# A message-passing layer on one core: the one-hots compare with a row of numbers in PSUM, and the places are counted in one bank

## The chip, the core and the metric

The kernel runs on one core of a Trainium2 chip. The metric is the time of one execution on the device, in microseconds. A core has TensorE (PE in the profile; PEld is its weight load), VectorE (DVE), ScalarE (ACT), GpSimd (POOL) and SyncE (SP), which run side by side and wait for each other through semaphores, and DMA queues that move data between HBM and SBUF. TensorE writes to PSUM, a small memory of eight banks of 512 float32 numbers in each of 128 partitions. VectorE and ScalarE read it; in this kernel GpSimd and the DMA queues work on SBUF and HBM alone.

## What is computed

The inputs are 12,500 nodes with 128 features and 400,000 edges, sorted by destination, each with 20 attributes and a weight. Here `src` is `idx_i`, by which the sums are taken, and `dst` is `idx_j`, whose row is fetched.

```
h   = relu(layernorm(x)) @ W_in2f.T
Wij = smu(edge_attr_20 @ W_f1.T + b_f1) @ W_f2.T + b_f2      # per edge, 128 wide
Wij = Wij * edge_weight[:, None]
msg = h[dst] * Wij
agg = segment_sum(msg, src, 12500)
out = x + smu(agg @ W_o1.T + b_o1) @ W_o2.T + b_o2
```

`smu(x)` is a smooth activation made of `x` and `x * erf(...)`; the kernel builds it from one Gelu and one multiply-add.

## The kernel before

The edges are padded to 784 **units** of 512 edges (4 tiles of 128). 112 units make a **round**, and there are 7 rounds. A node is in one of 112 **buckets** by its row number modulo 112. For each unit, messages are computed and scattered to HBM, sorted by bucket (`sorted_rows`); for each round and bucket, 640 sorted rows are loaded again one round later and summed by node on TensorE with a second one-hot (a **segment**; 784 of them, `SEG_LAG` = 120 units behind). A prologue makes `h`, a last part makes the output from `agg`.

What happens to a unit n, with the names of the profile:

- TensorE makes `p_z` (line 926), ScalarE its Gelu (583), VectorE `act` (762).
- VectorE makes `pick` (766), the one-hot with which TensorE fetches `h[dst]` from a window (`p_h`, 944); ScalarE weighs it into `hg` (594).
- VectorE makes `onehot` (`bucket_of`, 771): 4 tiles of 112 columns, the row of numbers 0 to 111 (`iota_bf`, bf16, SBUF) compared with each edge's bucket (`node_l`, SBUF). TensorE multiplies it with triangular matrices (`rank` and `counted`, 950 and 967), which adds to a running count in the bank `p_pos` where the next free place of each bucket stands. VectorE picks each edge's place out of it (`places`, 785) and adds a correction (`row_numbers`, 793, writes `row_idx`).
- TensorE makes `p_w` (931, 933), VectorE multiplies it with `hg` into `msg` (779).
- GpSimd issues four indirect DMAs (`scatter`, 491), one for each tile, that write `msg` to the rows `row_idx`. `msg` and `row_idx` have four slots (`RING`), so `row_idx` of unit n waits until the scatters of unit n-4 have landed.

For a segment, VectorE makes `seg_hot` (`bucket_hot`, 804): 5 times 112 columns, the same numbers as float32 (`iota`, SBUF) compared with the node number in the loaded rows (`seg`, SBUF). TensorE sums (976), VectorE adds to `agg` (815, in the first round 813).

The order on each engine is written out by hand in a function `step`, run for every unit; `beats` unrolls the first 12 units of each round and loops over the rest. On VectorE a step is `act`, `pick`, `onehot` of unit n; then of unit n-1 `places`, `seg_hot` of a segment, `row_idx`, `agg`, `msg` of unit n-1. Counts of odd and even rounds stand in two banks, `p_pos0` and `p_pos1`. When a round opens, TensorE finishes the old round's count in the old bank and seeds the new one (`rank` with `opens`, 957 to 963); VectorE reads the old bank's totals (`totals`, 796 to 799) once in each round, at the end of the third step.

The eight banks of PSUM are `p_z`, two of `p_w`, `p_h`, two of `p_pos`, two of `p_seg`. The two banks of `p_pos` are used again by the last layer (1030 to 1039, read at 880).

Of the kernel before, what the change touches and what calls it, by code (L numbers as in the profile page):

```python
# [64 lines left out]
def build(nc, n_nodes, n_edges, F, R, t):  # L65
# [27 lines left out]
    with ctx:  # L93
# [3 lines left out]
        def ps(name, shape, dt=F32):  # L97
            return ctx.enter_context(nc.psum_tensor(name, shape, dt))
# [79 lines left out]
        p_z = ps("p_z", [LANES, BANK])  # L178
        p_w = [ps(f"p_w{v}", [LANES, TILES_U, F]) for v in range(2)]
        p_h = ps("p_h", [LANES, TILES_U, F])  # L180
        p_pos = [ps(f"p_pos{v}", [LANES, BANK]) for v in range(2)]
        p_seg = [ps(f"p_seg{v}", [LANES, BANK]) for v in range(2)]

        s_x = sem("s_x")
# [5 lines left out]
        s_pool = sem("s_pool")  # L190
        s_pool2 = sem("s_pool2")
        s_seeds = sem("s_seeds")
        s_u16 = sem("s_u16")
        s_zeros = sem("s_zeros")
        s_zrow = sem("s_zrow")
# [451 lines left out]
        def _(dve):  # L647
# [76 lines left out]
            dve.tensor_scalar(w_o2[:, :], w_o2[:, :], SMU_W, None, ALU.mult).then_inc(s_scaled, 1)  # L724

            dve.wait_ge(s_pool, 5)
            dve.tensor_copy(seeds[0:1, :, :], iota_bf[0:1, :].unsqueeze(1).to_broadcast([1, BUFS, BUCKETS])).then_inc(s_seeds, 1)
            dve.wait_ge(s_win_ld, 32)
            link(dve.tensor_scalar(seed_row[:, :, :], seed_row[:, :, :], float(CAP), (CAP + FILLED) / 2, ALU.mult, ALU.add))
# [25 lines left out]

            loop(dve, phase_a, n_groups, 5)
            dve.wait_ge(s_win_row, 1)

            def smu(n, v):
                wait_for(dve, s_gelu, n, 1, 1)  # L760
# [7 lines left out]

            def bucket_of(n, slot):
                wait_for(dve, s_rank, n, 1, 2 - RING)  # L770
                dve.tensor_tensor(onehot[:, slot, :, :], iota_bf[:, :].unsqueeze(1).to_broadcast([LANES, TILES_U, BUCKETS]),  # L771
                                  node_l[:, bass.ds(n.value(TILES_U), TILES_U)].unsqueeze(2).to_broadcast([LANES, TILES_U, BUCKETS]),
                                  ALU.is_equal).then_inc(s_hot, 1)

# [6 lines left out]
            def places(n, v, slot, rnd):  # L781
                wait_for(dve, s_rank, n, 1, 1)
                wait_for(dve, s_idx, n, 1, -1)
                for k in range(TILES_U):
                    last = dve.tensor_tensor_reduce(out=product[:, k, :], in0=onehot[:, slot, k, :], in1=p_pos[rnd % 2][:, 0:BUCKETS],  # L785
                                                    scale=1.0, scalar=0.0, op0=ALU.mult, op1=ALU.add,
                                                    accum_out=place[:, v, k:k + 1])
                last.then_inc(s_place, 1)
# [6 lines left out]

            def totals(rnd):
                dve.wait_ge(s_total, rnd + 1)
                dve.tensor_tensor(counts[:, rnd, :], p_pos[rnd % 2][0:1, 0:BUCKETS], seed_row[:, rnd % BUFS, :], ALU.subtract
                                  ).then_inc(s_count, 1)

            def bucket_hot(m, v, slot, rnd, ld):
                wait_for(dve, s_segld[slot], ld, 16, 16)
                wait_for(dve, s_seg, m, 1, -1)
                dve.scalar_tensor_tensor(seg_hot[:, v, :, :], seg[:, slot, :, F:F + 1].to_broadcast([LANES, CAP_T, NODE_P]),  # L804
                                         -float(LANES * (rnd + 1)),
                                         iota[:, :].unsqueeze(1).to_broadcast([LANES, CAP_T, NODE_P]), ALU.add, ALU.is_equal
                                         ).then_inc(s_seghot, 1)

            def gather_sum(m, v, rnd, bucket):
# [7 lines left out]
            def step(st):  # L817
                if st.has() and st.v() == 0:
                    wait_for(dve, s_ends[st.q()], st.pair().over(2), 16, 16)
                if st.has():  # L820
                    smu(st.at(), st.v())
                    pick_target(st.at(), st.pair(), st.q(), st.v())
                    bucket_of(st.at(), st.ring())
                if st.has(1):
                    places(st.at(1), st.v(1), st.ring(1), st.rnd_of(1))
                if st.has_seg():
                    bucket_hot(st.seg_at(), st.v(), st.c % SEGS, st.seg_rnd(), st.seg_at().over(SEGS))
                if st.has(1):
                    row_numbers(st.at(1), st.v(1), st.ring(1))
                if st.has_seg(2):  # L830
                    gather_sum(st.seg_at(2), st.v(2), st.seg_rnd(2), st.bucket(2))
                if st.has(1):
                    message(st.at(1), st.v(1), st.ring(1))
                if st.i is None and st.c == 2 and st.rnd >= 1 and st.rnd <= rounds:
                    totals(st.rnd - 1)

            beats(dve, step, 2)

# [38 lines left out]
            def output(g, b, deep):  # L877
                wait_for(dve, s_om, g, 1, 1)
                wait_for(dve, s_xl[deep], g.over(DEEP), 48, 48)
                dve.tensor_tensor(x_out[:, deep, :, :], p_pos[b][0:NODE_P, :].rearrange("p (k n) -> p k n", k=NODE_G),  # L880
                                  x_out[:, deep, :, :], ALU.add).then_inc(s_of, 1)

            for c in range(n_groups + 1):
# [6 lines left out]
        def _(pe):  # L890
# [56 lines left out]

            def counted(slot, rnd):
                for k in range(TILES_U):
                    last = pe.matmul(p_pos[rnd % 2][:, 0:BUCKETS], not_before[:, :], onehot[:, slot, k, :], start=False, stop=False,  # L950
                                     skip_group_check=True)
                return last

            def rank(n, slot, rnd, opens):
                wait_for(pe, s_hot, n, 1, 1)
                wait_for(pe, s_place, n)
                if opens:
                    if rnd > 0:
                        counted((slot - 1) % RING, rnd - 1).then_inc(s_total, 1)
                    if rnd > 1:  # L960
                        pe.wait_ge(s_count, rnd - 1)
                    pe.matmul(p_pos[rnd % 2][:, 0:BUCKETS], step_rows[:, :], seeds[:, rnd % BUFS, :], start=True, stop=False,
                              skip_group_check=True)
                else:
                    counted((slot - 1) % RING, rnd)
                for k in range(TILES_U):
                    last = pe.matmul(p_pos[rnd % 2][:, 0:BUCKETS], before[:, :], onehot[:, slot, k, :], start=False, stop=False,
                                     skip_group_check=True)
                last.then_inc(s_rank, 1)

# [59 lines left out]
            def last_layer(g, b):  # L1030
                wait_for(pe, s_os, g, 1, 1)
                wait_for(pe, s_of, g, 1, -1)
                pe.matmul(p_pos[b][0:NODE_P, :], ones_bf[:, 0:NODE_P],
                          bias_rows[:, B_O2, :, :].rearrange("p k f -> p (k f)"), start=True, stop=False)
                for k in range(NODE_G):
                    last = pe.matmul(p_pos[b][0:NODE_P, k * F:(k + 1) * F],  # L1036
                                     hid[:, b, k * NODE_P:(k + 1) * NODE_P], w_o2[:, :],
                                     start=False, stop=(k == NODE_G - 1))
                last.then_inc(s_om, 1)
# [54 lines left out]
```

## Time and profile before

| | us |
|---|---|
| median of 3 runs | 4690.14 |
| lowest and highest | 4686.88 and 4690.92 |
| profiled execution | 4673.0 |
| its span, first to last instruction | 4671.3 |

The profile is of the one profiled execution, which was 17.1 us faster than the median. It has three stretches: the prologue to 343 us, where GpSimd's first scatter starts; the 784 units, until GpSimd's last scatter ends at 4421 us; and the rest, in which the last round's segments are loaded and summed and the output is made.

### The profile page before, as it was taken

How to read it: one execution, taken by the hardware profiler on the slowest of the kernel's cores; microseconds unless marked ns; L12 is line 12 of the kernel's file. 1: busy time of each engine (PE TensorE's matmuls, PEld its weight loads, DVE VectorE, ACT ScalarE, POOL GpSimd, SP SyncE). 2: the span in 40 equal slices, each digit the busy share in tenths (PEclk: the TensorE clock that was granted, in tenths of full speed). 3: DMA queues.
4: the chain of work that ended last, by engine and by line, in shares of the span. 5: the costliest groups of instructions: out<-in, count | busy, mean ns of one | idle time of the engine just before them, and what ended most of it. 6: DMA issues, size and time to landing. Idle time of an engine off the chain costs nothing.

```text
span 4671.3 us, 120335 instructions
## 1 busy us (share of the span) xinstructions
PE 3674.7 (79%) x32823; PEld 2929.2 (63%) x32823; DVE 3210.1 (69%) x12188; ACT 1518.5 (33%) x4903; POOL 3132.1 (67%) x3158
## 2 busy tenths in 40 slices
PE   0417777788888888888888888888888888888788
PEld 0305555566666666666666666666666666666676
DVE  6406556577777777777777777777777777777665
ACT  0603333333333333333333333333333333333201
POOL 0007777777777777777777777777777777777600
PEclk9759999999999999999999999999999999999999
DMA  8684333355555555555555555555555555555476
GB/s 191 180 189 126 94 96 94 104 156 157 156 155 158 158 159 155 158 158 158 156 155 158 157 155 157 154 155 157 159 156 156 154 158 157 158 156 154 149 216 187
DMA packets 373005, 720.26 MB, mean 154 GB/s; under 512 B 82062, under 2 KB 132900, under 8 KB 372346
## 3 DMA queue, kind: packets, MB, share of 16 engines
q1 hardware_dynamic: 246476, 456.19, 36.2%
q0 software_dynamic: 100352, 207.33, 12.7%
q10 hardware_dynamic: 26082, 55.61, 5.0%
q8 instruction: 44, 0.72, 0.1%
q14 instruction: 51, 0.42, 0.0%
HBM read 450.43 MB, written 268.35 MB: 154 GB/s over the span
## 4 chain that ended last, share of the span: by engine, by line
POOL 33%; DMA 24%; issue 22%; DVE 10%; ACTq 5%; PE 3%; ACT 1%; DVEq 1%; POOLq 1%; SPq 0%
POOL sorted_rows L491 33%; DMA sorted_rows<-msg,row_idx 21%; DVE msg L779 4%; ACTq L536 4%; DMA seg<-sorted_rows 2%; PE p_seg L976 1%; DVE product L785 1%; DMA x_all<-in_x 1%; DVE row_idx L793 1%; DVE onehot L771 1%; DVE agg L815 1%; DVE act L762 1%; POOLq L489 1%; DVE pick L766 1%; PE p_pos L1036 0%
## 5 line engine op out<-in xcount | busy, mean ns | idle before, releaser
L491 POOL DMA_INDIRECT sorted_rows<-msg,row_idx x3136 | 3121.9, 996 | 1249.3 <-issue 1142.3
L976 PE MATMUL p_seg<-seg_hot,seg 128*128 128x112 f32 x7840 | 1031.6, 280 | 323.6 <-DVE agg L815 273.1
L976 PEld LDWEIGHTS p_seg<-seg_hot,seg 128*128 128x128 f32 x7840 | 940.0, 192 | 395.9 <-issue 215.7
L926 PE MATMUL p_z<-attr,w_f 128*128 128x512 f32 x1568 | 862.9, 633 | 262.0 <-DVE act L762 232.7
L587 ACT ACTIVATE msg<-node_p 128x4 f32 (+1 forms) x784 | 163.8, 209 | 2492.9 <-DMA sorted_rows<-msg,row_idx 2492.8
L594 ACT ACTIVATE hg<-p_h,weight 128x128 f32<-128x128 f32 x3136 | 893.1, 373 | 86.5 <-PE p_h L944 58.4
L793 DVE TENSOR_TENSOR row_idx<-place,earlier 128x4 int32<-128x4 f32 x784 | 129.0, 165 | 1108.7 <-DMA sorted_rows<-msg,row_idx 1103.0
L933 PEld LDWEIGHTS p_w<-w_f,act 128*128 128x128 f32 x6272 | 826.9, 192 | 20.7
L933 PE MATMUL p_w<-w_f,act 128*128 128x128 f32 x6272 | 828.5, 275 | 0.0
L950 PEld LDWEIGHTS p_pos<-onehot,not_before 128*128 128x128 bf16 x3136 | 191.7, 98 | 849.1 <-DVE onehot L771 529.4
L944 PE MATMUL p_h<-win,pick 128*128 128x128 bf16 x9408 | 669.6, 222 | 4.1 <-DMA win<-h 4.1
L785 DVE CUSTOM_DVE_ANT_0 product<-onehot,p_pos 128x112 bf16<-128x112 bf16 x3136 | 657.4, 265 | 0.0
L762 DVE SCALAR_TENSOR_TENSOR act<-p_z,gelu 128x512 f32<-128x512 f32 x784 | 535.7, 683 | 160.4 <-ACT gelu L583 149.1
L804 DVE SCALAR_TENSOR_TENSOR seg_hot<-seg,iota 128x560 f32<-128x560 f32 x784 | 578.5, 738 | 84.7 <-DMA seg<-sorted_rows 72.8
L944 PEld LDWEIGHTS p_h<-win,pick 128*128 128x128 bf16 x9408 | 569.5, 100 | 4.5 <-DMA win<-h 4.5
L779 DVE TENSOR_TENSOR msg<-p_w,hg 128x512 f32<-128x512 f32 x784 | 536.5, 684 | 1.4 <-PE p_w L933 1.4
L950 PE MATMUL p_pos<-onehot,not_before 128*128 128x112 bf16 x3136 | 289.3, 216 | 251.0 <-DVE place L785 247.4
L583 ACT ACTIVATE gelu<-p_z 128x512 f32<-128x512 f32 x784 | 467.3, 596 | 59.0 <-issue 41.2
L771 DVE TENSOR_TENSOR onehot<-iota_bf,node_l 128x448 bf16<-128x448 bf16 x784 | 483.9, 617 | 0.0
L926 PEld LDWEIGHTS p_z<-attr,w_f 128*128 128x128 f32 x1568 | 238.8, 192 | 290.8 <-DVE act L762 254.9
L931 PE MATMUL p_w<-bias_rows,ones_bf 128*128 128x512 bf16 x784 | 299.3, 382 | 0.0
L766 DVE TENSOR_SCALAR pick<-ends,win_row 128x512 bf16<-128x512 uint16 x784 | 293.3, 374 | 0.0
(92 smaller groups left out, 1555.1 us busy)
## 6 DMA issues: line engine op xcount, KB each, us to landing
seg<-sorted_rows SPq DMA_DIRECT2D x784, 322.5 KB
ends<-ends SPq DMA_DIRECT2D x392, 256.0 KB
sorted_rows<-msg,row_idx POOLq DMA_INDIRECT x3136
sorted_rows<-zero_rows ACTq DMA_DIRECT2D x12, 3612.0 KB
win<-h SPq DMA_DIRECT2D x392, 96.0 KB
attr<-in_attrT SPq DMA_DIRECT2D x392, 80.0 KB
h<-h_parts SPq DMA_DIRECT2D x28, 336.0 KB, 2.7
x_all<-in_x SPq DMA_DIRECT2D x1, 5376.0 KB
```

The lines of the kernel that those rows point to most:

```text
L491: pool.indirect_dma_start(out=sorted_rows[:, :], out_offset=bass.IndirectOffsetOnAxis(ap=row_idx[:, slot, k:k + 1], axis=0), in_=msg[:, sl ...
L594: last = act.activation(hg[:, v, k, :], p_h[:, k, :], ACT.Copy, scale=weight[:, bass.ds(n.value(TILES_U, k), 1)])
L762: dve.scalar_tensor_tensor(act1[:, v, :], p_z[:, :], SMU_L, gelu[:, v, :], ALU.mult, ALU.add).then_inc(s_smu, 1)
L771: dve.tensor_tensor(onehot[:, slot, :, :], iota_bf[:, :].unsqueeze(1).to_broadcast([LANES, TILES_U, BUCKETS]), node_l[:, bass.ds(n.value(T ...
L779: dve.tensor_tensor(msg[:, slot, :, 0:F], p_w[v][:, :, :], hg[:, v, :, :], ALU.mult).then_inc(s_msg, 1)
L785: last = dve.tensor_tensor_reduce(out=product[:, k, :], in0=onehot[:, slot, k, :], in1=p_pos[rnd % 2][:, 0:BUCKETS], scale=1.0, scalar=0.0 ...
L804: dve.scalar_tensor_tensor(seg_hot[:, v, :, :], seg[:, slot, :, F:F + 1].to_broadcast([LANES, CAP_T, NODE_P]), -float(LANES * (rnd + 1)), ...
L926: pe.matmul(p_z[:, :], w_f1[:, :], attr[:, q, v * UNIT:(v + 1) * UNIT], start=True, stop=True).then_inc(s_z, 1)
L933: last = pe.matmul(p_w[v][:, k, :], act1[:, v, k * LANES:(k + 1) * LANES], w_f2[:, :], start=False, stop=(k == TILES_U - 1))
L944: last = pe.matmul(p_h[:, k, :], pick[:, v, k * LANES:(k + 1) * LANES], win[:, q, part * F:(part + 1) * F], start=(part == 0), stop=(part ...
L950: last = pe.matmul(p_pos[rnd % 2][:, 0:BUCKETS], not_before[:, :], onehot[:, slot, k, :], start=False, stop=False, skip_group_check=True)
L976: last = pe.matmul(p_seg[v][:, 0:NODE_P], seg[:, slot, k, 0:F], seg_hot[:, v, k, :], start=(k == 0), stop=(k == CAP_T - 1))
```

## The change

The two banks of `p_pos` become one bank `p_pos` and one bank `p_iota`. VectorE copies `iota` (float32) into `p_iota` once, in the prologue. `bucket_of` and `bucket_hot` read their row of numbers from `p_iota`, float32 in both; before, `bucket_of` read bf16. Their other operand stays where it was, as do their outputs.

With one bank for the count, TensorE may seed a new round only after VectorE has read the old totals: it waits for `s_count` at every opening of a round but the first, where before it waited for the totals of two rounds ago. VectorE takes the totals one step earlier, between `onehot` and `places` of that step. The last layer alternates between `p_z` and `p_pos`.

```diff
-        p_pos = [ps(f"p_pos{v}", [LANES, BANK]) for v in range(2)]
+        p_pos = ps("p_pos", [LANES, BANK])
+        p_iota = ps("p_iota", [LANES, BANK])
+        p_out = [p_z, p_pos]
...
             dve.wait_ge(s_pool, 5)
+            dve.tensor_copy(p_iota[:, 0:NODE_P], iota[:, :]).then_inc(s_iota, 1)
...
             dve.wait_ge(s_win_row, 1)
+            dve.wait_ge(s_iota, 1)
...
-                dve.tensor_tensor(onehot[:, slot, :, :], iota_bf[:, :].unsqueeze(1).to_broadcast([LANES, TILES_U, BUCKETS]),
+                dve.tensor_tensor(onehot[:, slot, :, :], p_iota[:, 0:BUCKETS].unsqueeze(1).to_broadcast([LANES, TILES_U, BUCKETS]),
                                   node_l[:, bass.ds(n.value(TILES_U), TILES_U)].unsqueeze(2).to_broadcast([LANES, TILES_U, BUCKETS]),
                                   ALU.is_equal).then_inc(s_hot, 1)
...
-                                         iota[:, :].unsqueeze(1).to_broadcast([LANES, CAP_T, NODE_P]), ALU.add, ALU.is_equal
+                                         p_iota[:, 0:NODE_P].unsqueeze(1).to_broadcast([LANES, CAP_T, NODE_P]), ALU.add, ALU.is_equal
                                          ).then_inc(s_seghot, 1)
...
                     bucket_of(st.at(), st.ring())
+                if st.i is None and st.c == 1 and 1 <= st.rnd <= rounds:
+                    totals(st.rnd - 1)
                 if st.has(1):
...
                     message(st.at(1), st.v(1), st.ring(1))
-                if st.i is None and st.c == 2 and st.rnd >= 1 and st.rnd <= rounds:
-                    totals(st.rnd - 1)
...
                     if rnd > 0:
                         counted((slot - 1) % RING, rnd - 1).then_inc(s_total, 1)
-                    if rnd > 1:
-                        pe.wait_ge(s_count, rnd - 1)
-                    pe.matmul(p_pos[rnd % 2][:, 0:BUCKETS], step_rows[:, :], seeds[:, rnd % BUFS, :], start=True, stop=False,
+                        pe.wait_ge(s_count, rnd)
+                    pe.matmul(p_pos[:, 0:BUCKETS], step_rows[:, :], seeds[:, rnd % BUFS, :], start=True, stop=False,
                               skip_group_check=True)
...
-                pe.matmul(p_pos[b][0:NODE_P, :], ones_bf[:, 0:NODE_P],
+                pe.matmul(p_out[b][0:NODE_P, :], ones_bf[:, 0:NODE_P],
```

On VectorE, where round 1 opens, the order before had the totals (`counts`) behind `msg` of the third step:

```order
L793 TENSOR_TENSOR row_idx<-place,earlier 128x4 [waits s_scat1,s_place]
L779 TENSOR_TENSOR msg<-p_w,hg 128x4x128 [waits s_scat1,s_w,s_hg]
L798 TENSOR_TENSOR counts<-p_pos,seed_row 1x112 [waits s_total]
L762 SCALAR_TENSOR_TENSOR act<-p_z,gelu 128x512 [waits s_w,s_gelu]
L766 TENSOR_SCALAR pick<-ends,win_row 128x512 [waits s_ph]
L771 TENSOR_TENSOR onehot<-iota_bf,node_l 128x448 [waits s_rank]
```

On VectorE at the same opening the changed kernel has them in the second step (its line numbers are five higher here):

```order
L767 SCALAR_TENSOR_TENSOR act<-p_z,gelu 128x512 [waits s_w,s_gelu]
L771 TENSOR_SCALAR pick<-ends,win_row 128x512 [waits s_ph]
L776 TENSOR_TENSOR onehot<-p_iota,node_l 128x448 [waits s_rank]
L803 TENSOR_TENSOR counts<-p_pos,seed_row 1x112 [waits s_total]
L790 ISA product,place<-onehot,p_pos 128x112 [waits s_idx,s_rank]
L790 ISA place 128x1
```

The totals moved ahead of the first `places` of the new round, and `onehot` reads `p_iota` in place of `iota_bf`.

On TensorE the instructions at the opening of round 1 were these:

```order
L926 MATMUL p_z<-attr,w_f 128x512 [waits s_smu]
L950 MATMUL p_pos<-onehot,not_before 128x112 [waits s_place,s_hot]
L950 MATMUL p_pos<-onehot,not_before 128x112 x3
L962 MATMUL p_pos<-seeds,step_rows 128x112
L967 MATMUL p_pos<-onehot,before 128x112 x4
L944 MATMUL p_h<-win,pick 128x128 [waits s_hg,s_pick,s_win0]
```

In the changed kernel they are, on the same engine and at the same place:

```order
L931 MATMUL p_z<-attr,w_f 128x512 [waits s_smu]
L955 MATMUL p_pos<-onehot,not_before 128x112 [waits s_place,s_hot]
L955 MATMUL p_pos<-onehot,not_before 128x112 x3
L966 MATMUL p_pos<-seeds,step_rows 128x112 [waits s_count]
L971 MATMUL p_pos<-onehot,before 128x112 x4
L949 MATMUL p_h<-win,pick 128x128 [waits s_hg,s_pick,s_win0]
```

No matmul moved; the seed got the wait for `s_count`, which VectorE's `counts` releases.

## Rows read from the trace of the kernel before

**Rows 1.** The page: each engine's busy time, share of the span, instructions.
```profile
PE 3674.7 (79%) x32823; PEld 2929.2 (63%) x32823; DVE 3210.1 (69%) x12188; ACT 1518.5 (33%) x4903; POOL 3132.1 (67%) x3158
```

**Rows 2.** GpSimd's scatters: the page's group, then the line's own view (ns min/median/max).
```profile
L491 POOL DMA_INDIRECT sorted_rows<-msg,row_idx x3136 | 3121.9, 996 | 1249.3 <-issue 1142.3
...
L491 POOL DMA_INDIRECT sorted_rows<-msg,row_idx x3136: 954/958/1590, 343.0 to 4419.8; - x196
```

**Rows 3.** Who waited for whom: total us, times, longest us.
```profile
POOL sorted_rows L491 <- issue: 1142.3, 2785, 293.5
DVE row_idx L793 <- DMA sorted_rows<-msg,row_idx: 1103.0, 617, 4.3
...
POOL sorted_rows L491 <- DVE msg L779: 105.8, 347, 0.3
```

**Rows 4.** Timeline, GpSimd and VectorE in one unit: start us, us, instruction.
```profile
2505.70 0.16 DVE L793 TENSOR_TENSOR row_idx<-place,earlier 128x4 int32<-128x4 f32 x1 [1.48 <-DMA sorted_rows<-msg,row_idx]
...
2506.65 0.68 DVE L762 SCALAR_TENSOR_TENSOR act<-p_z,gelu 128x512 f32<-128x512 f32 x1
...
2506.74 0.96 POOL L491 DMA_INDIRECT sorted_rows<-msg,row_idx  x1 [0.30 <-issue]
...
2507.25 0.55 DVE L766 TENSOR_SCALAR pick<-ends,win_row 128x512 bf16<-128x512 uint16 x1
...
2507.72 0.60 DVE L771 TENSOR_TENSOR onehot<-iota_bf,node_l 128x448 bf16<-128x448 bf16 x1
...
2508.01 1.15 POOL L491 DMA_INDIRECT sorted_rows<-msg,row_idx  x1 [0.30 <-issue]
...
2509.01 0.73 DVE L804 SCALAR_TENSOR_TENSOR seg_hot<-seg,iota 128x560 f32<-128x560 f32 x1
...
2509.46 1.12 POOL L491 DMA_INDIRECT sorted_rows<-msg,row_idx  x1 [0.30 <-issue]
```

**Rows 5.** Timeline: first and last scatter issue lengthened under onehot, then under seg_hot.
```profile
354.55 1.15 POOL L491 DMA_INDIRECT sorted_rows<-msg,row_idx  x1 [0.30 <-issue]
...
4388.02 1.15 POOL L491 DMA_INDIRECT sorted_rows<-msg,row_idx  x1 [0.30 <-issue]
...
939.15 1.11 POOL L491 DMA_INDIRECT sorted_rows<-msg,row_idx  x1 [0.30 <-issue]
...
4412.05 1.14 POOL L491 DMA_INDIRECT sorted_rows<-msg,row_idx  x1 [0.30 <-issue]
```

**Rows 6.** Timeline: the scatter issue that took longest, and pick beside it.
```profile
3829.09 0.33 DVE L766 TENSOR_SCALAR pick<-ends,win_row 128x512 bf16<-128x512 uint16 x1
3829.20 1.59 POOL L491 DMA_INDIRECT sorted_rows<-msg,row_idx  x1 [0.30 <-issue]
```

**Rows 7.** VectorE's groups: shapes, count, busy us, mean ns, idle before them.
```profile
L804 DVE SCALAR_TENSOR_TENSOR seg_hot<-seg,iota 128x560 f32<-128x560 f32 x784 | 578.5, 738 | 84.7 <-DMA seg<-sorted_rows 72.8 <-PE p_seg L976 11.6
L779 DVE TENSOR_TENSOR msg<-p_w,hg 128x512 f32<-128x512 f32 x784 | 536.5, 684 | 1.4 <-PE p_w L933 1.4
...
L771 DVE TENSOR_TENSOR onehot<-iota_bf,node_l 128x448 bf16<-128x448 bf16 x784 | 483.9, 617 | 0.0
L766 DVE TENSOR_SCALAR pick<-ends,win_row 128x512 bf16<-128x512 uint16 x784 | 293.3, 374 | 0.0
...
L746 DVE TENSOR_TENSOR h_parts<-hg,h_parts 112x512 bf16<-112x512 f32 x28 | 19.1, 682 | 0.1
...
L798 DVE TENSOR_TENSOR counts<-p_pos,seed_row 1x112 f32<-1x112 f32 x7 | 1.8, 252 | 0.0
```

**Rows 8.** Windows, round 0: GpSimd's scatter issues (line 491), then msg (779).
```profile
343.00:926.00 583.00, 444.57 (x455) 0.92 0.36 104
...
343.00:926.00 583.00, 80.06 (x116) 0.92 0.36 104
```

**Rows 9.** The chain that ended last, as the last scatter lands: start us, us, what.
```profile
4419.81 2.28 DMA sorted_rows<-msg,row_idx
4422.31 2.74 DMA seg<-sorted_rows
```

More of the change, by code:

```diff
@@ L192, in build @@
         s_seeds = sem("s_seeds")
+        s_iota = sem("s_iota")
         s_u16 = sem("s_u16")
@@ L784, in places @@
                 for k in range(TILES_U):
-                    last = dve.tensor_tensor_reduce(out=product[:, k, :], in0=onehot[:, slot, k, :], in1=p_pos[rnd % 2][:, 0:BUCKETS],
+                    last = dve.tensor_tensor_reduce(out=product[:, k, :], in0=onehot[:, slot, k, :], in1=p_pos[:, 0:BUCKETS],
                                                     scale=1.0, scalar=0.0, op0=ALU.mult, op1=ALU.add,
@@ L797, in totals @@
                 dve.wait_ge(s_total, rnd + 1)
-                dve.tensor_tensor(counts[:, rnd, :], p_pos[rnd % 2][0:1, 0:BUCKETS], seed_row[:, rnd % BUFS, :], ALU.subtract
+                dve.tensor_tensor(counts[:, rnd, :], p_pos[0:1, 0:BUCKETS], seed_row[:, rnd % BUFS, :], ALU.subtract
                                   ).then_inc(s_count, 1)
@@ L879, in output @@
                 wait_for(dve, s_xl[deep], g.over(DEEP), 48, 48)
-                dve.tensor_tensor(x_out[:, deep, :, :], p_pos[b][0:NODE_P, :].rearrange("p (k n) -> p k n", k=NODE_G),
+                dve.tensor_tensor(x_out[:, deep, :, :], p_out[b][0:NODE_P, :].rearrange("p (k n) -> p k n", k=NODE_G),
                                   x_out[:, deep, :, :], ALU.add).then_inc(s_of, 1)
@@ L949, in counted @@
                 for k in range(TILES_U):
-                    last = pe.matmul(p_pos[rnd % 2][:, 0:BUCKETS], not_before[:, :], onehot[:, slot, k, :], start=False, stop=False,
+                    last = pe.matmul(p_pos[:, 0:BUCKETS], not_before[:, :], onehot[:, slot, k, :], start=False, stop=False,
                                      skip_group_check=True)
@@ L966, in rank @@
                 for k in range(TILES_U):
-                    last = pe.matmul(p_pos[rnd % 2][:, 0:BUCKETS], before[:, :], onehot[:, slot, k, :], start=False, stop=False,
+                    last = pe.matmul(p_pos[:, 0:BUCKETS], before[:, :], onehot[:, slot, k, :], start=False, stop=False,
                                      skip_group_check=True)
@@ L1032, in last_layer @@
                 wait_for(pe, s_of, g, 1, -1)
-                pe.matmul(p_pos[b][0:NODE_P, :], ones_bf[:, 0:NODE_P],
+                pe.matmul(p_out[b][0:NODE_P, :], ones_bf[:, 0:NODE_P],
                           bias_rows[:, B_O2, :, :].rearrange("p k f -> p (k f)"), start=True, stop=False)
                 for k in range(NODE_G):
-                    last = pe.matmul(p_pos[b][0:NODE_P, k * F:(k + 1) * F],
+                    last = pe.matmul(p_out[b][0:NODE_P, k * F:(k + 1) * F],
                                      hid[:, b, k * NODE_P:(k + 1) * NODE_P], w_o2[:, :],
```

## The prediction

> **What bounds the kernel now.** I read the engines' busy time first [rows 1]. It names nobody: PE is busy for 79% of the span, DVE for 69%, POOL for 67%. The idle time before each engine's work tells more. The scatter line of GpSimd [rows 2] has 3121.9 us of work and 1249.3 us of idle time, which looks like slack. But one wait of that idle time is 293.5 us long [rows 3], the wait for the first unit. What is left is 955.8 us before 3135 issues, 0.305 us before each, and every timeline row shows this same 0.30 [rows 4, 5]. In the timeline of the whole trace the shortest gap is 0.30 and the longest 0.32. So between 343 us and the end of the last scatter at 4421 us GpSimd never waits for data: it needs 0.30 us before each issue, whatever the other engines do. The 347 gaps that are put down to VectorE's `msg` are 105.8 / 347 = 0.30 us too, the same fixed gap.
>
> VectorE and ScalarE wait for GpSimd instead. `row_idx` waited 1103 us for the scatters to land [rows 3], since a slot is free only when the scatters of four units ago have landed. The queue between them is full: at 926 us VectorE had finished 116 messages and GpSimd had begun 455 issues, 113.75 units [rows 8]. That is 2.25 units, at 5.2 us a unit some 11.7 us, by which GpSimd's data are early.
>
> So the middle of the kernel lasts as long as GpSimd's 3136 issues: 3121.9 + 955.8 = 4078 us of the span of 4671.3, or 5.20 us for a unit. What changes an issue's duration changes the time one to one. What changes the work of the other engines changes nothing until a unit takes one of them more than 5.2 us.
>
> **How long an issue must take.** The shortest is 954 ns, the median 958, the mean 996, the longest 1590 [rows 2]. Most are thus at one value, and few are lengthened much. At 0.956 us each they would take 2998 us; 124 us are on top. I asked which VectorE instruction ran at the moment when each issue began. In rows 4 `onehot` runs from 2507.72 to 2508.32; an issue begins at 2508.01 and takes 1.15 us in place of 0.96, so its end is put off by 0.19 us. `seg_hot` runs from 2509.01 to 2509.74, an issue begins at 2509.46 and takes 1.12. In both, what is added is the time to the end of VectorE's instruction less 0.12. The issue at 2506.74, which begins beside `act`, takes 0.96.
>
> The same over the whole timeline, first and last of the lengthened ones in rows 5: 285 issues began under `onehot`, all of them lengthened, by 245 ns on average, 69.9 us in sum. 403 began under `seg_hot`, 302 of these visibly lengthened, by 115 ns on average over the 403, 46.4 us in sum. 52 began under `pick`, 3.4 us in sum. 489 began under `act`, 370 under the product of `places` and 218 under `msg`, and were longer by 1 to 2 ns. `onehot` and `seg_hot` have both of their inputs in SBUF; `act`, `msg` and the product have one in SBUF and one in PSUM. (`row_idx` has both in SBUF too, but with 0.16 us [rows 4] it is nearly over before the 0.12 are.) The duration of VectorE's instruction is not what matters, since `msg` with 684 ns is longer than `onehot` with 617 [rows 7]. I read it thus: GpSimd must read its row numbers from SBUF at the start of an issue, and cannot while VectorE reads two inputs from there.
>
> The Trainium skill has this rule, with a part that speaks against this change (SBUF — State Buffer, Who interferes with whom). It says that a VectorE instruction with two SBUF inputs contends with a GpSimd instruction that reads SBUF, but also that `tensor_tensor` did not stall DMAs issued by GpSimd, since descriptor generation wants the write side (there marked as inferred). By the second sentence the sum below would be zero and the time stay at 4690; the 285 lengthened issues of this trace stand against it, and I go by them.
>
> **The change, part by part.**
>
> `onehot` and `seg_hot` get one input in PSUM, as `act` and `msg` have. Their 285 and 403 meetings with an issue should then cost what those of `act` and `msg` cost: nearly nothing. That is -69.9 - 46.4 = -116.3 us, on GpSimd's path, all of it in the end of the kernel.
>
> Their own duration: the trace has no such comparison out of PSUM. The nearest rows are two 512-wide float32 instructions, `msg` with one input in PSUM and 684 ns, `h_parts` with both in SBUF and 682 [rows 7]. So I take +2 ns for each, and as a far bound twice the time per element: (738 - 617) / (560 - 448) = 1.08 ns more for each of 1008 elements, +1.09 us a unit. VectorE has this room, nearly: in rows 4 a unit of its own work runs from `row_idx` at 2505.70 to the end of `seg_hot` at 2509.74, 4.04 us, against GpSimd's floor of 4 x (0.956 + 0.305) = 5.04. With +2 ns it is hidden behind GpSimd. With +1.09 it would be 5.13, 0.09 over the floor. `onehot` read bf16 before and was no faster for it: 617 ns for 448 elements lies on the same line as `seg_hot` in float32, so going to float32 costs nothing.
>
> `pick` stays. It is a one-input instruction and holds an issue up now and then [rows 6], the longest of all at 1.59 us, where `onehot` came right behind it. What of that is `pick`'s remains. When the others no longer push the issues about, more issues may begin under it. If they fell at random, 4 x 0.34 / 5.04 of the units would have one, 211 in place of today's 52 (124 with those where it overlaps a neighbour). At the mean of 65 ns that is 14 us; below zero it can go only by the 3.4 it costs now. I take +3.
>
> The opening of a round: TensorE's seed waits for the totals, which come behind `act`, `pick` and `onehot` of the next unit: 0.68 + 0.37 + 0.62 + 0.25 = 1.9 us [rows 7], and VectorE's `places` then waits for the seed and four small matmuls, below 1 us. Behind TensorE's wait stand the fetch `p_h` and `p_w` of that unit, so ScalarE's `hg` and VectorE's `msg` come up to 3 us late. This happens six times, and each time GpSimd has 11.7 us of work in front of it, which VectorE can refill at 4.04 against 5.04 us a unit. Cost 0; if the cover were gone, 6 x 3 = 18 us. Taking the totals a step earlier is the same 252 ns, hidden too.
>
> The copy into `p_iota` is one instruction before the first unit, below 0.3 us. The last layer has the same matmuls and the same read in `p_z` instead of a second `p_pos`: 0. The last part begins when the last scatter has landed [rows 9] and waits for loads; it keeps its 250 us.
>
> **Sum.** The profiled execution took 4673.0. 4673.0 - 116.3 + 3 = 4560. The median of the runs is 17 us above the profiled execution, and no row says why. If that is time outside the issues, it stays and gives 4577. If those runs had more of the lengthened issues, it goes as well and gives 4560. I take 4576.
>
> **Rivals.**
> - *Pick takes over.* VectorE's phase against GpSimd is set by the landing of GpSimd's own scatters, so `pick` could come to lie on the start of an issue in every unit. For it: `pick` lengthens issues. Against: `pick` starts at all phases between two issues. Price 784 x 0.065 = 51 us, at most some 100; time about 4628.
> - *The hold is not relieved.* What holds GpSimd might not be the second SBUF input but something that stays, such as the broadcast of a short row over several tiles, which only these two have. Then the change does what it says and gains nothing: 4690. Against: `pick` holds issues too, without such a broadcast.
> - *Slower: VectorE becomes the bound.* If a comparison out of PSUM took well over twice the time per element, VectorE's unit would pass 5.20 us. It decides from +1.16 us a unit on; at three times the time per element it is 4.04 + 2.18 = 6.22, and 784 x 1.02 = 800 us slower, about 5490. Against: the 2 ns between `msg` and `h_parts`.
> - *The openings show.* 18 us on top, 4595; it lies within the range.
>
> **How the numbers follow.** Forecast, with the openings' case: 0.88. Pick takes over 0.05, hold not relieved 0.05, VectorE the bound 0.02. The range is 4556 (the 17 us go too, and `pick` costs no more than now) to 4600 (they stay, `pick` costs 11 more, half the openings' price shows). About 0.2% can be told from no change here. Faster by more than that: the forecast and pick's case, 0.93; within 0.2%: 0.05; slower: 0.02.
>
> **What would show it.** Right: the scatter line's mean falls from 996 to about 960 ns and its busy time to some 3010 us, the gaps stay at 0.30, and issues that begin under `onehot` and `seg_hot` take 0.96. `onehot` and `seg_hot` stay near 617 and 738 ns. VectorE waits for the scatters' landing about as long as before, less what the unit loses. Wrong: issues of 1.1 us still under these two; a gap over 0.32 us before an issue, above all where a round opens; many more issues lengthened under `pick`; `row_idx` no longer waiting for landings, which would make VectorE the bound.

## The result, and the profile after

| | before | changed kernel |
|---|---|---|
| median of the runs, us | 4690.23 (4 runs) | 4561.66 (4 runs, 4557.97 to 4564.18) |
| profiled execution, us | 4673.0 | 4564.2 |
| its span, us | 4671.3 | 4562.4 |

The ratio is 0.9727, with a 95% interval of 0.971 to 0.9743: 128.6 us less between the medians, 108.9 us less between the two spans. The time lies in the forecast range, 14 us below the forecast of 4576.

The scatter line, first as the page of the changed kernel has it and then in the line's own view (it is line 494 now), answers to [rows 2]:

```profile
L494 POOL DMA_INDIRECT sorted_rows<-msg,row_idx x3136 | 3006.6, 959 | 1249.9 <-issue 1180.7
...
L494 POOL DMA_INDIRECT sorted_rows<-msg,row_idx x3136: 954/958/1136, 343.9 to 4305.7; - x196
```

The mean fell from 996 to 959 ns and the longest from 1590 to 1136. Busy time fell by 115.3 us; idle time before the issues is 1249.9 as it was 1249.3. In the timeline no gap between two issues is above 0.32 us. So the middle of the kernel still lasts as long as GpSimd's issues, and each of them takes less. (A row of this view reads min/median/max in ns, then the first and last start in us.)

One unit of the timeline, GpSimd and VectorE, answers to [rows 4]:

```profile
2502.22 0.35 DVE L771 TENSOR_SCALAR pick<-ends,win_row 128x512 bf16<-128x512 uint16 x1
...
2502.49 0.61 DVE L776 TENSOR_TENSOR onehot<-p_iota,node_l 128x448 bf16<-128x448 f32 x1
...
2502.78 0.96 POOL L494 DMA_INDIRECT sorted_rows<-msg,row_idx  x1 [0.30 <-issue]
...
2503.78 0.73 DVE L809 SCALAR_TENSOR_TENSOR seg_hot<-seg,p_iota 128x560 f32<-128x560 f32 x1
...
2504.04 0.96 POOL L494 DMA_INDIRECT sorted_rows<-msg,row_idx  x1 [0.30 <-issue]
```

The issue at 2502.78 begins 0.29 us into `onehot`, as the one in [rows 4] did, and takes 0.96 in place of 1.15. The one at 2504.04 begins under `seg_hot` and takes 0.96 in place of 1.12. I grouped all 3136 issues of each trace by the VectorE instruction that ran when they began, as in the prediction:

| issues that began under | before: count, us on top of 0.956 each | changed kernel |
|---|---|---|
| `onehot` | 285, 69.9 | 404, 0.7 |
| `seg_hot` | 403, 46.4 | 487, 0.9 |
| `pick` | 52, 3.4 | 60, 3.0 |
| all | 3136, 123.9 | 3136, 8.6 |

More issues than before begin under the two one-hots, and it costs nothing. (VectorE's records overlap by up to 0.08 us; an issue counts for the instruction whose own part it falls in. Twelve issues of the kernel before that began within the first 0.02 us of an `onehot` record are left out by this, and none of them was lengthened. "Lengthened" means over 1.01 us.)

VectorE's groups (line, operation, shapes, count, busy us and mean ns, idle before) answer to [rows 7]:

```profile
L809 DVE SCALAR_TENSOR_TENSOR seg_hot<-seg,p_iota 128x560 f32<-128x560 f32 x784 | 573.5, 732 | 85.7 <-DMA seg<-sorted_rows 78.0 <-PE p_seg L980 7.4
L784 DVE TENSOR_TENSOR msg<-p_w,hg 128x512 f32<-128x512 f32 x784 | 536.1, 684 | 9.3 <-ACT hg L597 2.8 <-PE p_w L938 2.5 <-issue 2.0
...
L776 DVE TENSOR_TENSOR onehot<-p_iota,node_l 128x448 bf16<-128x448 f32 x784 | 480.9, 613 | 0.0
L771 DVE TENSOR_SCALAR pick<-ends,win_row 128x512 bf16<-128x512 uint16 x784 | 301.9, 385 | 0.0
```

Out of PSUM and in float32, `onehot` takes 613 ns where it took 617, `seg_hot` 732 where it took 738. `pick` rose from 374 to 385: it is the one that waits for GpSimd more often now.

The view of the totals' line says what the one bank costs where a round opens:

```profile
L803 DVE TENSOR_TENSOR counts<-p_pos,seed_row x7: 252/252/253, 893.6 to 4289.2; 1x112 f32<-1x112 f32 x7
...
  PEld p_pos L966: 20.5, 6
  PE p_pos L966: 19.5, 6
```

Its second part lists who waited for the totals: the seed's weight load six times, 20.5 us in sum, 3.4 us each on average, and the seed's matmul beside it. None of this reaches GpSimd. VectorE and TensorE at the opening of round 1 show what the wait is made of:

```profile
891.42 0.16 DVE L798 TENSOR_TENSOR row_idx<-place,earlier 128x4 int32<-128x4 f32 x1 [1.15 <-DMA sorted_rows<-msg,row_idx]
...
891.55 0.69 DVE L784 TENSOR_TENSOR msg<-p_w,hg 128x512 f32<-128x512 f32 x1
892.16 0.68 DVE L767 SCALAR_TENSOR_TENSOR act<-p_z,gelu 128x512 f32<-128x512 f32 x1
...
893.61 0.25 DVE L803 TENSOR_TENSOR counts<-p_pos,seed_row 1x112 f32<-1x112 f32 x1
893.91 0.10 PEld L966 LDWEIGHTS p_pos<-seeds,step_rows 128*128 128x128 bf16 x1 [3.21 <-DVE counts L803]
```

TensorE had finished the old count at 890.94. VectorE first had to wait for a landing and then make `msg` of the unit before; `act` began only after that, at 892.16.

The window of round 0, first GpSimd's issues and then `msg`, answers to [rows 8]:

```profile
343.00:926.00 583.00, 441.84 (x461) 0.90 0.37 106
...
343.00:926.00 583.00, 80.92 (x117) 0.90 0.37 106
```

The window leaves out the first message, which ended before 343 us. With it VectorE had finished 118 messages at 926 us, against 461 / 4 = 115.25 units begun: it is 2.75 units ahead. (In the kernel before it was 2.25: one message more than the 116 of [rows 8] had begun, and 116 were finished.) `row_idx` waited 970.7 us for landings in the whole execution (1103.0 before, [rows 3]).

### The profile page after: what moved, and what is told of

Read it like the earlier page. It is cut to its first block, busy times and chain, and to the rows that moved or that the text cites. A ratio compares the mean times of both kernels' runs of the same rounds, so it can differ in the third digit from the quotient of the medians.

```text
span 4562.4 us, 120337 instructions
## 1 busy us (share of the span) xinstructions
PE 3655.7 (80%) x32823; PEld 2939.1 (64%) x32823; DVE 3207.0 (70%) x12189; ACT 1521.3 (33%) x4903; POOL 3016.7 (66%) x3158
## 4 chain that ended last, share of the span: by engine, by line
POOL 39%; issue 28%; DMA 17%; DVE 6%; ACTq 5%; PE 3%; POOLq 1%; ACT 1%; DVEq 0%; SPq 0%
POOL sorted_rows L494 39%; DMA sorted_rows<-msg,row_idx 13%; ACTq L539 4%; DVE msg L784 3%; DMA seg<-sorted_rows 2%; PE p_seg L980 1%; DMA x_all<-in_x 1%; POOLq L492 1%; DVE row_idx L798 0%; ACTq L546 0%; DVE agg L820 0%; DVE product L790 0%; DVE onehot L776 0%; DMA x_out<-in_x 0%; DVE act L767 0%
## 5 line engine op out<-in xcount | busy, mean ns | idle before, releaser
L494 POOL DMA_INDIRECT sorted_rows<-msg,row_idx x3136 | 3006.6, 959 | 1249.9 <-issue 1180.7
L938 PEld LDWEIGHTS p_w<-w_f,act 128*128 128x128 f32 x6272 | 836.9, 194 | 21.2
L798 DVE TENSOR_TENSOR row_idx<-place,earlier 128x4 int32<-128x4 f32 x784 | 128.2, 164 | 974.3 <-DMA sorted_rows<-msg,row_idx 970.7
L809 DVE SCALAR_TENSOR_TENSOR seg_hot<-seg,p_iota 128x560 f32<-128x560 f32 x784 | 573.5, 732 | 85.7 <-DMA seg<-sorted_rows 78.0
L776 DVE TENSOR_TENSOR onehot<-p_iota,node_l 128x448 bf16<-128x448 f32 x784 | 480.9, 613 | 0.0
```

Of the source, the lines that this page charges most:

```text
L494: pool.indirect_dma_start(out=sorted_rows[:, :], out_offset=bass.IndirectOffsetOnAxis(ap=row_idx[:, slot, k:k + 1], axis=0), in_=msg[:, sl ...
L776: dve.tensor_tensor(onehot[:, slot, :, :], p_iota[:, 0:BUCKETS].unsqueeze(1).to_broadcast([LANES, TILES_U, BUCKETS]), node_l[:, bass.ds(n. ...
L938: last = pe.matmul(p_w[v][:, k, :], act1[:, v, k * LANES:(k + 1) * LANES], w_f2[:, :], start=False, stop=(k == TILES_U - 1))
```

## The experiments

Every kernel was run beside the kernel before on the same chip, and ratios are to that. The chips differed in a way that I had not reckoned with. On the chip of the next two sections the kernel before took 4687 to 4690 us (medians), as in the runs of the forecast and of the result. On three others the same program took 6035 to 6170 us; GpSimd is not the bound there. No chip was seen at both speeds, so whether the chip or something else at the time makes the difference is not shown. The experiments of the first kind come first.

### Holding GpSimd again, with an instruction that nobody needs

`hold_early` is the changed kernel with one VectorE instruction more in each unit, in the place and of the length of `onehot`, with both inputs in SBUF and no broadcast:

```diff
+        scratch = sb("scratch", [LANES, 2, TILES_U, BUCKETS])
...
+                    dve.tensor_tensor(scratch[:, st.v(), :, :].rearrange("p k f -> p (k f)"), ones_bf[:, 0:TILES_U * BUCKETS],
+                                      bias_rows[:, 0:1, :, :].rearrange("p a k f -> p (a k f)")[:, 0:TILES_U * BUCKETS], ALU.add)
                     bucket_of(st.at(), st.ring())
```

> The changed kernel, both one-hots out of PSUM, with one more VectorE instruction for each unit, ahead of onehot: two plain bf16 rows of SBUF added into a scratch row that nobody reads. It stands where onehot stood in time, so issues begin under it: some 400, lengthened by 320 ns, 130 us in sum, against 38 to 41 us where it stood behind onehot. On a chip where before takes 6035 to 6170 us: if less holding is what costs there, it gives back most of the 3.4%: 1.005 to 1.015 of before; if reading out of PSUM costs, it stays at 1.03. On a chip where before takes 4690: 0.973 and up to 130 us, 1.00 of before.

Measured: 4691.61 us, 1.0005 of before (0.9995 to 1.0014). The whole gain is gone. The page's scatter line:

```profile
L495 POOL DMA_INDIRECT sorted_rows<-msg,row_idx x3136 | 3138.4, 1001 | 1250.8 <-issue 1190.4
```

and one meeting in its timeline:

```profile
2501.98 0.61 DVE L829 TENSOR_TENSOR scratch<-ones_bf,bias_rows 128x448 f32<-128x448 bf16 x1
2502.27 1.15 POOL L495 DMA_INDIRECT sorted_rows<-msg,row_idx  x1 [0.30 <-issue]
2502.51 0.61 DVE L777 TENSOR_TENSOR onehot<-p_iota,node_l 128x448 bf16<-128x448 f32 x1
```

486 issues began under the new instruction, all of them lengthened, by 275 ns on average, 133.8 us in sum (expected were 400 with 320 ns). 218 began under `onehot`, which reads PSUM, and took 0.3 us more in sum.

`psum_early` is the control: the same place and length, but one of the two inputs in PSUM.

```diff
+                    dve.tensor_tensor(scratch[:, st.v(), :, :], p_iota[:, 0:BUCKETS].unsqueeze(1).to_broadcast([LANES, TILES_U, BUCKETS]),
+                                      node_l[:, bass.ds(st.at().value(TILES_U), TILES_U)].unsqueeze(2).to_broadcast([LANES, TILES_U, BUCKETS]),
+                                      ALU.is_equal)
                     bucket_of(st.at(), st.ring())
```

> The changed kernel with one more VectorE instruction for each unit, ahead of onehot: the comparison out of PSUM (p_iota with node_l) into a scratch row that nobody reads. It has the place of hold_early's instruction and about its length, but one of its inputs is in PSUM. On a chip where before takes 4690 us: theory (only two SBUF inputs hold GpSimd) 0.973 of before, as the changed kernel; rival (hold_early lost the gain by 0.6 us more VectorE work a unit, not by the place of its inputs) 1.000. On a chip where before takes 6035 to 6170 us and the changed kernel 1.034 of it: if reading out of PSUM is what costs there, 1.045 to 1.05; if it is that issues are no longer held up, 1.03 to 1.037.

Measured: 4565.33 us, 0.974 of before (0.9717 to 0.9763), as the changed kernel. Scatter line and a meeting:

```profile
L495 POOL DMA_INDIRECT sorted_rows<-msg,row_idx x3136 | 3009.4, 960 | 1250.1 <-issue 1173.3
...
2504.32 0.62 DVE L829 TENSOR_TENSOR scratch<-p_iota,node_l 128x448 f32<-128x448 f32 x1
2504.85 0.61 DVE L777 TENSOR_TENSOR onehot<-p_iota,node_l 128x448 bf16<-128x448 f32 x1
2504.87 0.96 POOL L495 DMA_INDIRECT sorted_rows<-msg,row_idx  x1 [0.30 <-issue]
```

303 issues began under this instruction and took 0.5 us more in sum. So 0.6 us more of VectorE's work in a unit costs nothing when one input is in PSUM, though it has the broadcast; with both inputs in SBUF and no broadcast it costs 126 us. That settles both the mechanism and the rival of the broadcast.

The hold follows one rule in all eleven traces that have such a meeting. In 4591 issues that were lengthened under `onehot`, `seg_hot` or a scratch instruction with both inputs in SBUF, what an issue took above 0.956 us is the time from its start to the end of VectorE's instruction, less 0.125 us; the largest departure from this is 0.02 us.

### The holds back, and one instruction more

`psum_extra` has both one-hots back in SBUF, the count in one bank, and one comparison out of PSUM more, behind `onehot`:

```diff
-                dve.tensor_tensor(onehot[:, slot, :, :], p_iota[:, 0:BUCKETS].unsqueeze(1).to_broadcast([LANES, TILES_U, BUCKETS]),
+                dve.tensor_tensor(onehot[:, slot, :, :], iota_bf[:, 0:BUCKETS].unsqueeze(1).to_broadcast([LANES, TILES_U, BUCKETS]),
...
-                                         p_iota[:, 0:NODE_P].unsqueeze(1).to_broadcast([LANES, CAP_T, NODE_P]), ALU.add, ALU.is_equal
+                                         iota[:, 0:NODE_P].unsqueeze(1).to_broadcast([LANES, CAP_T, NODE_P]), ALU.add, ALU.is_equal
...
                     bucket_of(st.at(), st.ring())
+                    dve.tensor_tensor(scratch[:, st.v(), :, :], p_iota[:, 0:BUCKETS].unsqueeze(1).to_broadcast([LANES, TILES_U, BUCKETS]),
+                                      node_l[:, bass.ds(st.at().value(TILES_U), TILES_U)].unsqueeze(2).to_broadcast([LANES, TILES_U, BUCKETS]),
+                                      ALU.is_equal)
```

> Both one-hots read from SBUF (as in banks_only, 1.000 of before), and one more VectorE instruction for each unit, behind onehot: the same comparison out of PSUM (p_iota with node_l), into a scratch row that nobody reads. On a chip where before takes 6035 to 6170 us, where the changed kernel was 3.4% slower, two theories: if reading the row out of PSUM is what costs there, this is 1.01 to 1.016 of before; if what costs there is that GpSimd's issues are no longer held up, it stays at 1.000 to 1.005, since onehot and seg_hot still hold them (the scratch instruction holds none). On a chip where before takes 4690: 1.000 in both, or more where more issues begin under onehot and seg_hot.

Measured: 4758.65 us, 1.0138 of before (1.0119 to 1.0156).

```profile
L495 POOL DMA_INDIRECT sorted_rows<-msg,row_idx x3136 | 3206.0, 1022 | 1250.0 <-issue 1165.3
```

This is 69 us more than before, where I had expected 1.000 unless more issues met the one-hots. The scratch instruction itself held nothing (340 issues began under it, 0.5 us in sum). But it moved what came behind it: 334 issues began under `onehot` with 295 ns each (98.6 us; before 285 with 245) and 315 under `seg_hot` with 326 ns each (102.6 us, where before it was 403 with 115). The count of meetings hardly changed (649 and 688); what changed is how much of VectorE's instruction was still to come when the issue began. An instruction that holds nothing itself thus cost 69 us through the phase of the others.

The five traces of this kind of chip give one sum:

| kernel | span | scatter busy | difference |
|---|---|---|---|
| before | 4671.3 | 3121.9 | 1549.4 |
| changed | 4562.4 | 3006.6 | 1555.8 |
| `psum_early` | 4564.2 | 3009.4 | 1554.8 |
| `hold_early` | 4693.9 | 3138.4 | 1555.5 |
| `psum_extra` | 4760.9 | 3206.0 | 1554.9 |

What is not an issue's duration is 1555 us in the four changed ones, whatever else differs, and 6 us less in the profiled execution of before. In all of them the gaps before the issues are 956 us in sum. The 6 us lie behind the last issue (250.5 us before, 254.0 to 255.8 in the four) and ahead of the first (343.0 and 343.9 to 345.1). The last part varies as much with one and the same kernel: 250.2, 255.6 and 256.5 us in the three traces of `hot_sbuf` further down. On this account the one bank costs nothing that shows; it was not timed by itself on such a chip.

### The other kind of chip

The one bank by itself was `banks_only`:

```diff
-                dve.tensor_tensor(onehot[:, slot, :, :], p_iota[:, 0:BUCKETS].unsqueeze(1).to_broadcast([LANES, TILES_U, BUCKETS]),
+                dve.tensor_tensor(onehot[:, slot, :, :], iota_bf[:, 0:BUCKETS].unsqueeze(1).to_broadcast([LANES, TILES_U, BUCKETS]),
...
-                                         p_iota[:, 0:NODE_P].unsqueeze(1).to_broadcast([LANES, CAP_T, NODE_P]), ALU.add, ALU.is_equal
+                                         iota[:, 0:NODE_P].unsqueeze(1).to_broadcast([LANES, CAP_T, NODE_P]), ALU.add, ALU.is_equal
```

> The count in one bank and the totals a step earlier, but both one-hots read their numbers from SBUF as before. Theory: the one bank costs nothing, since GpSimd has more than 11 us of work in front of it at each opening: 4690 within 0.1%. Rival (the later seeds show): up to 18 us more, 4708. Rival (the one bank gave part of the gain): below 4680.

Measured: 6046.43 us where before took 6040.95, 1.0001 (0.9986 to 1.0015). The one bank costs nothing that shows here either, though GpSimd no longer has messages waiting for it. Its page:

```profile
PEclk9677778788888888888888888888888888888899
...
L494 POOL DMA_INDIRECT sorted_rows<-msg,row_idx x3136 | 3183.7, 1015 | 2562.5 <-DVE msg L784 1405.1
```

GpSimd waits 1405 us for messages. The granted clock of TensorE is 7 to 8 tenths in nearly every slice of the units; in the kernel before of the forecast it was 9 there. The timeline shows TensorE itself without a wait that the profile knows (columns as before, idle time in brackets):

```profile
3004.95 0.10 PEld L955 LDWEIGHTS p_pos<-onehot,not_before 128*128 128x128 bf16 x1 [1.33 <-issue]
3005.66 0.21 PE L955 MATMUL p_pos<-onehot,not_before 128*128 128x112 bf16 x1 [1.22 <-issue]
3006.36 0.14 PEld L955 LDWEIGHTS p_pos<-onehot,not_before 128*128 128x128 bf16 x2 [1.32 <-issue]
```

Weight loads and matmuls come one at a time here, 0.70 us from each to the next, where four weight loads take 0.23 us together in other places. In the whole trace 888 records of TensorE's weight load (PEld) come more than 0.45 us after the end of the one ahead of them without a semaphore to wait for, 703 us in sum, and 578 of SyncE's; in the traces of the forecast and of the changed kernel it is 4 or 5 on PEld. What withholds the instructions I don't know. They are only a part of the lost time: TensorE's own busy time is 4388.5 us, against 3674.7 for as many instructions in the trace before, at a granted clock of 0.835 against 0.968.

The two reads were put back into SBUF one at a time. In `hot_sbuf` it is that of `onehot`, here from the float32 row (the kernel before read the bf16 one):

```diff
-                dve.tensor_tensor(onehot[:, slot, :, :], p_iota[:, 0:BUCKETS].unsqueeze(1).to_broadcast([LANES, TILES_U, BUCKETS]),
+                dve.tensor_tensor(onehot[:, slot, :, :], iota[:, 0:BUCKETS].unsqueeze(1).to_broadcast([LANES, TILES_U, BUCKETS]),
```

> The changed kernel, with the row of numbers of onehot read from SBUF again, as float32 (seg_hot still reads it from PSUM). Theory (a VectorE instruction with two SBUF inputs puts off the start of a scatter issue): in the changed kernel 404 issues begin under onehot, before it was 285; at the 245 ns that such a meeting cost before, 70 to 99 us come back: 4632 to 4661 us, with no issue lengthened under seg_hot. Rival (the gain came from the count in one bank or from something else than the place of the row of numbers): stays at 4562.

> The row of numbers of onehot from SBUF, seg_hot's from PSUM, as in hot_sbuf. Where GpSimd is the bound: theory 0.988 to 0.994 of before (4632 to 4661 us), issues under onehot lengthened by some 245 ns and none under seg_hot; rival (the gain was not the place of the row) 0.973.

> The row of numbers of onehot from SBUF, seg_hot's from PSUM, as in hot_sbuf. On a chip where before takes some 4690 us and GpSimd never waits for a message: theory 0.988 to 0.994 of before (4632 to 4661 us); rival (the gain was not the place of the row) 0.973. On a chip like those of the first two groups (before 6035 to 6041 us): 1.011 to 1.016 again, with issues lengthened under onehot alone.

In `seg_sbuf` it is that of `seg_hot`:

```diff
-                                         p_iota[:, 0:NODE_P].unsqueeze(1).to_broadcast([LANES, CAP_T, NODE_P]), ALU.add, ALU.is_equal
+                                         iota[:, 0:NODE_P].unsqueeze(1).to_broadcast([LANES, CAP_T, NODE_P]), ALU.add, ALU.is_equal
```

> The changed kernel, with the row of numbers of seg_hot read from SBUF again (onehot still reads it from PSUM). Theory: 403 to 487 issues begin under seg_hot, at 115 ns each 46 to 56 us come back: 4608 to 4618 us, with no issue lengthened under onehot. Rival (onehot's was the only hold that counted): 4562. If the two holds shift each other's meetings, this run and the one with onehot in SBUF do not add up to 129 us.

> The row of numbers of seg_hot from SBUF, onehot's from PSUM, as in seg_sbuf. Where GpSimd is the bound: theory 0.983 to 0.985 of before (4608 to 4618 us), issues under seg_hot lengthened by some 115 ns and none under onehot; rival 0.973.

`extra_two` adds `hold_early`'s instruction behind `onehot` instead of ahead of it:

> The changed kernel with one more VectorE instruction for each unit, behind onehot: it adds two bf16 rows of SBUF of 448 elements, both plain rows without a broadcast, into a float32 scratch row that nobody reads. VectorE's own work goes from 4.04 to 4.7 us a unit, still under the 5.04 of four issues. Theory (two SBUF inputs hold GpSimd, whatever their form): it meets 285 to 404 issues at 245 ns, 70 to 99 us more: 4632 to 4661 us, and issues that begin under it are lengthened to its end less 0.12. Rival (it was the broadcast of a short row that held GpSimd): 4562.

> The changed kernel with one more addition of two plain bf16 rows of 448 elements in SBUF for each unit, behind onehot, whose result nobody reads, as in extra_two. Where GpSimd is the bound: theory (two SBUF inputs hold GpSimd, broadcast or not) 0.988 to 0.994 of before; rival (it was the broadcast) 0.973, with no issue lengthened under it.

And the changed kernel itself:

> The changed kernel itself beside the kernel before, on the chip of this group of runs. On a chip where GpSimd's issues are the bound (before near 4690 us, gaps before an issue never over 0.32 us): 0.973 of before again. On a chip like that of the first group, where before took 6041 us and GpSimd waited 1.4 ms for messages, the shorter issues lie on no path: 0.99 to 1.01 of before there; if the two reads out of PSUM cost something of their own, 1.02, since each of them alone with the other in SBUF was at 1.011.

All of these ran on such chips. The table has the ratios to before on the same chip, the sum of what issues took on top of 0.956 us each, and the sum of the late records of PEld, in the order of the runs:

| kernel | ratios (95% interval of the first) | issues on top, us | late records, us |
|---|---|---|---|
| `banks_only` | 1.0001 (0.9986 to 1.0015) | 186 | 703 |
| `seg_sbuf` | 1.0114 (1.0091 to 1.0138), 1.0126 | 122, 139 | 774, 739 |
| `hot_sbuf` | 1.0113 (1.0086 to 1.014), 1.0162, 1.0084 | 162, 153, 155 | 863, 818, 923 |
| `extra_two` | 1.0298 (1.0252 to 1.0345), 1.0295 | 48, 50 | 976, 976 |
| changed, `after_2` | 1.034 (1.0284 to 1.0396) | 20 | 1005 |

These runs could not show what each read is worth where GpSimd is the bound, since there they never ran; 69.9 and 46.4 us of the trace before remain its only split. What they do show is the hold, apart from the time. In `hot_sbuf` 452 of 456 issues that began under `onehot` were lengthened (337 ns on average) and none of 373 under `seg_hot`. In `seg_sbuf` none of 406 under `onehot` were, and 258 of 274 under `seg_hot`. In `extra_two` 161 of 188 under the plain addition were, and none of 402 under `onehot`.

They also show the change slower: by 3.4% on a chip where before took 6035 us, though its issues took 166 us less than those of `banks_only`. (The kernel before was not traced on such a chip; `banks_only`, at 1.0001 of it, stands for it.) With only one of the two reads out of PSUM it was 0.8 to 1.6% slower. The late records are more in the slower kernels, by 302 us between `banks_only` and `after_2`, though not in step within the three runs of `hot_sbuf`. Here is the scatter line of `after_2`, and what ScalarE waited for most in it (`remote` is a releaser that the profile cannot name):

```profile
L494 POOL DMA_INDIRECT sorted_rows<-msg,row_idx x3136 | 3018.0, 962 | 2910.2 <-DVE msg L784 1729.8
...
ACT hg L597 <- remote: 2081.4, 356, 9.6
```

Whether the read out of PSUM or the fact that GpSimd is held less calls this up was to be told by `psum_extra`, `hold_early` and `psum_early`, but these ran on a chip of the first kind. `extra_two` has 28 and 30 us of the hold back, and its 1.030 against the 1.034 of the changed kernel is within the intervals. So the cause of the slowdown stays open.

## Why the prediction was right

- **GpSimd is the bound, one to one.** Right: idle time before the issues unchanged to 0.6 us, span down by 108.9 with 115.3 us less of issues; the rest is 5.3 us more behind the last issue, 0.9 us ahead of the first and 0.3 us of gaps. The table of five spans shows it best.
- **-69.9 - 46.4 us for the two holds.** Right: 1.6 us of the 116.3 are left. The cause is shown by `hold_early` and `psum_early`, and by the issues of `hot_sbuf` and `seg_sbuf`, where only the place of one operand differs. That the hold lasts to the end of VectorE's instruction less 0.12 us holds in every trace with such a meeting. That it is the read of the row numbers which is held is not shown.
- **The duration out of PSUM, +2 ns taken.** A little off: -4 and -6 ns. It changes nothing.
- **Pick, +3 us taken for new meetings.** Off by more than the whole: its cost did not rise but went from 3.4 to 3.0. In `psum_early`, where the phases differ, it was 6.6, with 125 issues. So the term moves with the phase, within the bounds given.
- **The openings, 0.** Right on the path: no gap before an issue above 0.32 us. The wait was 2.8 to 4.6 us, 3.4 on average, against the 1.9 forecast for it. `act`, `pick`, `onehot` and the totals took 1.7 us of it, as counted. What I had left out is that VectorE is not yet at `act` when TensorE is done with the old count: it began `act` 0.9 to 2.8 us later, behind `row_idx` and `msg` of the unit before, and in four of the six openings `row_idx` had waited 0.8 to 1.7 us for a landing. That costs nothing in the end, since GpSimd had messages enough.
- **The last part keeps its 250 us.** Nearly: from the last issue's end to the span's end it was 250.5 us and is 255.8. Together with 0.9 us at the start and 0.3 us of gaps that is 6.5 us more, and the issues took 2.0 us less than forecast (115.3 saved, where 116.3 - 3 = 113.3 were counted). The two make up the 4.4 us between the forecast by spans, 4559.7 less 1.7, and the 4562.4 measured.
- **The 17 us between median and profiled execution.** This was the one term without a row, and it carries the whole miss. The forecast put the median 16 us above the profiled execution; it lies 2.5 us below. That is 19 us, of which the 4.4 above take back a part and leave 14. That the time lies in the range all the same is due to its lower end, which was drawn for this case. Where the 17 us of before came from is not shown. If all its runs had the 1555 us outside the issues, 6 of the 17 are the shorter rest of its profiled execution, and the other 11 are more held issues: 4688.5 - 1555 gives 3133.5 us of issues against the 3121.9 of the profile. That is an estimate.
- **The rivals.** Pick did not take over. That the hold stays through the broadcast is refuted. VectorE did not become the bound: `row_idx` still waits 971 us for landings, and `psum_early` shows room for 0.6 us more in a unit. What I had not thought of is that the change is slower on another chip, where TensorE's instructions come late.

## What to carry to other kernels

Where GpSimd issues DMAs without a pause, look at the duration of each issue beside VectorE's timeline: here one that began under an instruction with two inputs in SBUF took longer by what was left of that instruction less 0.125 us, and moving one of the inputs to a PSUM bank took the hold away at no cost in VectorE's time. If no bank is free, it is worth counting how much of VectorE's instruction is still to come when an issue begins, since merely shifting the phases cost 69 us in `psum_extra`. And run a change on more than one chip: this one was worth 2.7% where GpSimd was the bound and cost 3.4% where TensorE's instructions came late.

## What the runs showed of the hardware

- The same program took 4687 to 4690 us on some chips and 6035 to 6170 us on three others, steadily within each (6029.6 to 6061.8 in 13 runs of one). On the slow ones many of TensorE's and SyncE's instructions came about 0.70 us apart, and the granted clock of the whole execution was 0.82 to 0.85 against 0.96 to 0.98.
- An indirect scatter of 128 rows takes GpSimd 0.958 to 0.962 us (medians) and 0.305 us of gap on either kind of chip. It begins by something that a VectorE instruction with two SBUF inputs keeps from happening until 0.125 us before that instruction ends. This something lies at the very start: the twelve issues that began within 0.02 us of the start of an `onehot` record went ahead unheld in the kernel before, and there it was `onehot` that took longer, 0.655 to 0.677 us in place of 0.62.
- VectorE's one-input `pick` also waits the other way round: where it begins 0.4 to 0.7 us after an issue began, it takes 0.41 to 0.50 us on average in place of 0.344, in both kernels.
- A comparison with an input in PSUM as float32 is no slower than one out of SBUF: 613 against 617 ns for 448 columns, 732 against 738 for 560.
